# Graph layer 0: gather x itself, put the dense work beside the last quads, write the weighted one-hots on VectorE

## What is computed

```python
qk = x @ Wqk + bqk
v = x @ Wv + bv
scores = jnp.sum(qk[dst] * qk[src], axis=-1) / jnp.sqrt(jnp.float32(D))
scores = jnp.clip(scores, -5.0, 5.0)
e = jnp.exp(scores - m[dst])
s = jax.ops.segment_sum(e, dst, num_segments=N)
attn = e / s[dst]
out = jax.ops.segment_sum(attn[:, None] * v[src], dst, num_segments=N)
out = out @ Wo + bo
h = out + x
...
return gamma * (h - mu) / jnp.sqrt(var + 1e-05) + beta
```

## Time and profile before

| | us |
|---|---|
| three runs | 3143.76 (median), 3142.85, 3181.03 |
| the profiled execution: its own time | 3180.83 |
| its span | 3179.0 |
| first gather of layer 0 / its first score | 50.89 / 67.00 |
| last gather of layer 0 issued | 1297.58 |
| first load of the dense stage | 1312.32 |
| first gather of layer 1 | 1468.88 |

### The profile page before, as it was taken

One profiled execution on the slowest core, in us unless ns is written; L12 is line 12 of the kernel. 1 busy time (PEld: TensorE's weight loads), 2 busy tenths in 40 slices (PEclk: granted clock), 3 DMA queues, 4 the chain that ended last, 5 costly groups with the idle time before them and its releaser, 6 DMA issues. The chain is left out here.

```text
span 3179.0 us, 56851 instructions
## 1 busy us (share of the span) xinstructions
PE 2260.2 (71%) x15187; PEld 1822.2 (57%) x15187; DVE 1546.5 (49%) x6430; ACT 1040.5 (33%) x2916; POOL 1719.9 (54%) x1751
## 2 busy tenths in 40 slices
PE   4666667667667666554677777777777777777879
PEld 4666666657666566543455555555555555555656
DVE  4444444444444444595244444444444444444566
ACT  0222222222222222242244344344344344344443
POOL 2666666666666666445545545545545545545312
PEclk8988888898898988786788888878888878888879
DMA  6555555555555555224444444444444444444301
GB/s 216 159 151 154 152 154 152 153 154 152 154 151 153 153 153 152 68 73 119 132 126 124 127 126 122 129 123 124 129 125 123 129 123 127 127 124 126 109 15 37
DMA packets 443720, 413.11 MB, mean 130 GB/s; under 512 B 72747, under 2 KB 374571, under 8 KB 443532
## 3 DMA queue, kind: packets, MB, share of 16 engines
q1 hardware_dynamic: 356380, 233.60, 26.0%
q0 software_dynamic: 66560, 163.68, 19.3%
q10 hardware_dynamic: 20592, 13.63, 1.3%
HBM read 393.41 MB, written 17.25 MB: 129 GB/s over the span
## 5 line engine op out<-in xcount | busy, mean ns | idle before, releaser
L831 POOL DMA_INDIRECT rows<-xl_tab,src_cols x832 | 800.7, 962 | 730.2 <-DVE message L988 496.7
L254 POOL DMA_INDIRECT rows<-qkv_tab,src_cols x832 | 819.6, 985 | 477.8 <-remote 227.0
L301 PE MATMUL tile_sums<-gather,rows 128*128 128x128 f32 x1664 | 402.6, 330 | 395.3 <-issue 382.9
L301 PEld LDWEIGHTS tile_sums<-gather,rows 128*128 128x128 f32 x1664 | 308.3, 231 | 440.7 <-issue 438.8
L333 DVE CUSTOM_DVE_ANT_0 product<-rows,q_dst 128x128 f32<-128x128 f32 x832 | 234.4, 282 | 626.4 <-remote 567.0
L1001 DVE SCALAR_TENSOR_TENSOR node_sums<-node_sums,shrunk,tile_sums 128x128 f32 x832 | 282.0, 339 | 393.0 <-remote 358.0
L897 PEld LDWEIGHTS z_ps<-spread,window 128*128 128x128 f32 x1664 | 259.5, 215 | 222.6 <-issue 202.1
L303 PE MATMUL tile_sums<-gather,ones 128*128 128x128 f32 x1664 | 380.9, 317 | 0.0
L264 ACT ACTIVATE weight<-clipped 128x4 f32<-128x4 f32 x208 | 42.7, 205 | 954.6 <-issue 590.2
L342 DVE TENSOR_TENSOR node_sums<-node_sums,tile_sums 128x256 f32 x832 | 351.2, 422 | 4.8 <-PE tile_sums L303 1.6
L897 PE MATMUL z_ps<-spread,window 128*128 128x128 f32 x1664 | 272.2, 298 | 93.5 <-issue 88.9
(11 more groups left out here) (154 smaller groups left out, 2626.7 us busy)
## 6 DMA issues: line engine op xcount, KB each, us to landing
rel_bc<-rel_rows SPq DMA_DIRECT2D x416, 128.0 KB
window<-qkv_tab SPq DMA_DIRECT2D x832, 64.0 KB
attr<-in_attrT SPq DMA_DIRECT2D x208, 256.0 KB
window<-xr_tab SPq DMA_DIRECT2D x832, 64.0 KB
rows<-qkv_tab,src_cols POOLq DMA_INDIRECT x832
rows<-xl_tab,src_cols POOLq DMA_INDIRECT x832
qkv_tab<-qkv ACTq DMA_DIRECT2D x13, 512.0 KB, 5.4
xT<-in_xT SPq DMA_DIRECT2D x13, 256.0 KB, 5.1
```

The source lines that it names most:

```text
L254: nc.gpsimd.indirect_dma_start(out=rows[:, q * QT + i, :], out_offset=None, in_=qkv_tab, in_offset=bass.IndirectOffsetOnAxis(ap=src_cols[: ...
L301: nc.tensor.matmul(bank[:, i % 2, 0, :], rows[:, q * QT + i, P:], gather1[:, q % 2, i, :], start=True, stop=True)
L831: nc.gpsimd.indirect_dma_start(out=rows[:, r, i, :], out_offset=None, in_=xl_tab, in_offset=bass.IndirectOffsetOnAxis(ap=src_cols[:, tile: ...
```

## The change

- POOL gathers rows of x, an input (128 floats), into a ring of eight quads; so it can start before any table is made. It waits for `summed`, now raised twice a quad.
- The score of an edge is x[src] . p[dst] + c[dst]. `p_tab` holds p and c, 129 floats a node, from the weights multiplied together once at the start. Windows are 128 x 129.
- The sums are of weighted rows of x; Wv and Wo, multiplied together, are applied later (`w_vo`).
- `onehot_ps` and ACT's scaling are gone. DVE writes `gather1` from `iota_row`, `rel_cols` and the weight in one operation per tile.
- Layer 0 is written out in full on all engines, in steps T. Step T scores quad T, makes the one-hots of T-1 and adds the sums of T-2. `p_dst` and `tile_sums` have one buffer for each half of a quad.
- The table is made in the same block, four blocks ahead of the quads, with ACT copying.
- The dense work of block b begins at step 199 + b. It projects by `w_vo`, with the weights turned by four one-column products; two normalisations stay there; the middle one is folded into the last for the tables (eps changes), and x1 itself is scaled by ACT in layer 1 (`norm_x1`), after the ninth quad, a block a quad.
- In layer 1, several semaphores of DVE's chain are one.

The diff, cut to its core:

```diff
-    qkv_tab = nc.dram_tensor("qkv_tab", (NP, 2 * P), F32).ap()
+    p_tab = nc.dram_tensor("p_tab", (NP, P + 1), F32).ap()
...
+    AHEAD0 = 8
+    SLOTS = 4
+    DENSE = 199
...
+                for Q in range(quads):
+                    r = Q % AHEAD0
+                    if Q >= AHEAD0:
+                        pool.wait_ge(summed, 2 * (Q - AHEAD0 + 1))
+                    for i in range(QT):
+                        tile = Q * QT + i
+                        nc.gpsimd.indirect_dma_start(
+                            out=rows[:, r, i, :], out_offset=None, in_=t["x"],
...
+                def spread_p(Q, k):
+                    if k == 0:
+                        pe.wait_ge(spread_made, Q + 1)
+                        pe.wait_ge(window_in[Q % SLOTS], (Q // SLOTS + 1) * (QT + 1) * DMA)
+                    if Q:
+                        pe.wait_ge(scored, 2 * (Q - 1) + k + 1)
...
+                def add_up(Q, k):
+                    if k == 0:
+                        pe.wait_ge(onehot_made, Q + 1)
+                    if Q:
+                        pe.wait_ge(added, (Q - 1) * QT + 2 * k + 2)
...
+                for T in range(steps):
+                    for k in range(2):
+                        if T + 1 < quads:
+                            spread_p(T + 1, k)
+                        if 0 <= T - 1 < quads:
+                            add_up(T - 1, k)
+                    if T + QUADS < node_groups:
+                        make_p(T + QUADS)
+                    b = T - DENSE
...
+                    if 0 <= b < blocks:
+                        project(b)
+                    if 0 <= b - 5 < blocks:
+                        turn_v(b - 5)
+                        tables(b - 5)
...
+                def make_onehots(Q):
+                    dve.wait_ge(weighted, Q + 1)
...
+                        o = nc.vector.tensor_scalar(gather1[:, Q % 2, i, :], iota_row[:], rel_cols[:, tile:tile + 1],
+                                                    weight[:, Q % 2, i:i + 1], ALU.is_equal, ALU.mult)
...
+                def residual(b):
+                    n = block_tiles(b)
+                    dve.wait_ge(projected, b + 1)
+                    nc.vector.reciprocal(share[:, 0:n], t_ps[:, 0, 0:n]).then_inc(inverted, 1)
...
+                        o = nc.vector.scalar_tensor_tensor(h[:, b % 2, i, :], o_ps[:, i, :], share[:, i:i + 1],
+                                                           x_nm[:, b % QT, i, :], ALU.mult, ALU.add)
...
+                    if T < quads:
+                        clip(T)
...
+                    if 0 <= b - 1 < blocks:
+                        shift0(b - 1)
+                    if 0 <= b - 4 < blocks:
+                        shift1(b - 4)
+                    if 0 <= b < blocks:
+                        residual(b)
+                    if 0 <= b - 3 < blocks:
+                        moments1(b - 3)
+                    if 0 <= b < blocks:
+                        moments0(b)
...
+                def norm_x1(b):
+                    for i in range(block_tiles(b)):
+                        at = b * QT + i
+                        nc.scalar.activation(x1[:, b, i, :], x1[:, b, i, :], ACT.Identity, bias=shift1[:, at:at + 1],
```

More of the change, by code:

```diff
@@ L203, in build @@
[L203 to L211 removed]
+        w_in = sb("w_in", [P, 2, P])
@@ L235, in _ @@
             def _(sp):
-                def body(j, first, last):
-                    for q in range(QUADS):
-                        if not first:
-                            sp.wait_ge(q_spread, j * QUADS + q - QUADS + 1)
-                        sp.dma_start(rel_bc[:, q, :], rel_rows[bass.ds(j * QUADS + q, 1), :].to_broadcast([P, QW])
-                                     ).then_inc(window_in[q], DMA)
-                        for i, base in enumerate(window_bases(sp, j, q), q * QT):
-                            sp.dma_start(window[:, i, :], qkv_tab[bass.ds(base, P), 0:P]).then_inc(window_in[q], DMA)
@@ new lines, in spread_p @@
+                def spread_p(Q, k):
[4 more added lines that the diff above has]
+                        pe.wait_ge(scored, 2 * (Q - 1) + k + 1)
+                    for i in range(2):
+                        at = (2 * k + i) * P
+                        mm = nc.tensor.matmul(p_dst[k][:, i, 0:P + 1], spread[:, Q % 2, at:at + P],
+                                              window[:, Q % SLOTS, 2 * k + i, :], start=True, stop=True)
+                    mm.then_inc(p_spread, 1)
@@ new lines, in add_up @@
+                def add_up(Q, k):
[3 more added lines that the diff above has]
+                        pe.wait_ge(added, (Q - 1) * QT + 2 * k + 2)
+                    for i in range(2):
+                        nc.tensor.matmul(tile_sums[k][:, i, 0, :], rows[:, Q % AHEAD0, 2 * k + i, :],
+                                         gather1[:, Q % 2, 2 * k + i, :], start=True, stop=True)
+                        mm = nc.tensor.matmul(tile_sums[k][:, i, 1, :], ones[:], gather1[:, Q % 2, 2 * k + i, :],
@@ L304, in add_up @@
                                               start=True, stop=True)
                     mm.then_inc(summed, 1)
-                spread_q(0, 0, True)
-                def body(j, first, last):
-                    for q in range(QUADS):
-                        if q < QUADS - 1:
-                            spread_q(j, q + 1, first and q == 0)
-                        elif not last:
-                            spread_q(j + 1, 0)
-                        add_up(j, q, first and q < 2)
-                groups_of(pe, groups, body)
@@ L504, in tables @@
                 def tables(b):
[L506 removed]
+                    pe.wait_ge(hT_made, b + 1)
                     if b:
[L508 to L514 removed]
@@ L515, in _ @@
-                all_steps([(0, project), (3, turn_v), (-1, spread_inverse), (-2, turn_weights), (3, tables)])
+                        pe.wait_ge(lr_kept, b)
+                    for i in range(block_tiles(b)):
+                        nc.tensor.matmul(lr_ps[i // 2][:, i % 2, :], hT[:, i, :], w_lr[:], start=True, stop=False)
+                        mm = nc.tensor.matmul(lr_ps[i // 2][:, i % 2, :], ones[0:1, :], b_lr[:], start=False, stop=True)
+                    mm.then_inc(lr_made, 1)
+                pe.wait_ge(w_loaded, 6 * DMA)
@@ new lines, in _ @@
+                nc.tensor.matmul(lr_ps[0][0:1, 0, P:P + 1], b_in[:, 0:1], b_in[:, 0:1], start=True, stop=True)
+                nc.tensor.matmul(t_ps[:, 2, :], w_turned[:, 1, :], w_out[:], start=True, stop=True)
+                nc.tensor.matmul(lr_ps[0][0:1, 1, 0:P], b_in[:, 1:2], w_out[:], start=True, stop=True).then_inc(m_made, 1)
+                pe.wait_ge(m_kept, 4)
+                for b in range(QUADS):
+                    make_p(b)
+                spread_p(0, 0)
+                spread_p(0, 1)
@@ new lines, in score @@
+                def score(Q, k):
+                    dve.wait_ge(p_spread, 2 * Q + k + 1)
+                    if k == 0:
+                        dve.wait_ge(gathered[Q % AHEAD0], (Q // AHEAD0 + 1) * QT * DMA)
+                        if Q >= 2:
+                            dve.wait_ge(clip_done, Q - 1)
+                    for i in range(2):
+                        o = nc.vector.tensor_tensor_reduce(product[:, 2 * k + i, :], rows[:, Q % AHEAD0, 2 * k + i, :],
+                                                           p_dst[k][:, i, 0:P], 1.0, p_dst[k][:, i, P:P + 1], ALU.mult,
+                                                           ALU.add, scores[:, Q % 2, 2 * k + i:2 * k + i + 1])
+                    o.then_inc(scored, 1)
@@ L674, in build @@
+                dve.wait_ge(added, tiles)
     attention = ExitStack()
@@ L884, in _ @@
                         raise_falls(s)
+                    if Q >= LAG and Q - LAG < blocks:
+                        norm_x1(Q - LAG)
             @block.tensor
```

949 lines of the change are left out of this document (449 added, 500 removed).

## The result

| | before, us | after, us |
|---|---|---|
| median, runs | 3160.94, 4 | 3318.81, 4 (3317.32 to 3327.51) |
| ratio, 95% interval | | 1.0503, 1.0416 to 1.0591 |
| profiled execution / its span | 3180.83 / 3179.0 | 3319.3 / 3317.5 |
| exponential of quads 0 / 9 / 199 (ACT) | 68.2 / 118.7 / 1261.1 | 63.6 / 172.0 / 1301.2 |
| us a quad, quads 20 to 199 | 6.01 | 5.95 |

The four runs of the kernel before lie at 3143 and at 3180 us and its profiled execution is one of the upper pair, which is why the medians are 158 us apart and the two spans 138.

The account below looks back on a forecast made before the run. Gathers holding PE's signals, plus POOL's restart, bound layer 0's loop. Layer 1 starting 64 us earlier, less 10 inside it, gives 54 of 3180.83 (1.7%), which scales the median 3143.76 to 3090; range 3020 to 3200.

Parts of the forecast that it names:

- What bounds the loop: Layer 0's edges: PE's signals wait for POOL's gathers, 1.44 us each; four and a restart make 6.00, forecast 6.05 a quad.
- The 0.05: Layer 0's loop: us a quad added for one-hots on DVE lengthening the gathers beside them, taken between 0 and 0.14.
- the rival of the port: Layer 0's quads: one-hots and gathers fight for a port; 3357 at the locked price, 3190 in milder form; chance 0.20.
- The start: Before layer 0's loop: 32 gathers to 50 us, then table work; first score at 62, ninth quad of gathers about 70.
- 200 quads remain: Loop's end in layer 0: after the ninth quad's gathers at 70, quads at 6.05 each; last burst at 1274.
- The dense work beside quads: Steps 202 to 209, no gathers: eight steps of 10.5 us, 84 in all, to 1376.
- some 2 us: Dense work beside quads: DVE's wait in a step for PE's projection, whose matmuls were put at 0.9.
- The tail: Steps 210 and 211 at 6 us each, then the last block's chain of 16.8; layer 1 starts at 1405.
- The 2.9: Tail: us for the tables in the last block's chain, from 37.3 over 13 blocks.
- Layer 1: Layer 1: `norm_x1` gives ACT 1.65 us in each of 13 quads; could cost 21 or nothing, 10 taken.
- half-paying overlap: Rival: dense steps wait on held or late signals, 14 us not 10.5, and 21 in layer 1; +40, 3129; chance 0.15.

Follow-up runs that it names:

- e9: The changed kernel with POOL gathering three tiles of each quad, not four, from the ninth quad on; 3094.97 us, loop 4.68 us a quad.
- e11: The changed kernel with exponential ahead of copies, no one-row bias products, projection first, dense work from step 210, ring of four quads; 3183.58 us, loop 6.01.
- jobs 1 and 4: Two of five groups of runs, each on one chip; the kernel before took 2502 and 2507 us there, in the others 3177 to 3193.
- e4: The changed kernel with the exponential ahead of the table copies in ACT's order; 2586.99 us, start 61.8 us.
- e7: The changed kernel with the projection ahead of the step's products in PE's order; 3295.30 us, dense part 255 us.
- e5: The kernel before, unchanged, run again for its trace; 3189.22 us.
- e6: The changed kernel, unchanged, run again for its trace; 3354.10 us, in a job where the kernel before took 3193.17.
- e12: The changed kernel with exponential ahead of copies and both biases on DVE, projection still behind the step's products; 3200.23 us, dense part 210 us.
- e1: The changed kernel with the dense blocks from step 210 on, behind all quads; 2632.34 us where the kernel before took 2502.12.
- job 5: A group of runs on one chip, where the kernel before took 3177.18 us.

## Why the prediction was wrong

The forecast of 3090 missed by 229 us, and the sign. Some 36 of these lie between the median that it starts from (3143.76) and the profiled execution (3180.83); the rest, 192, is that layer 1 started 201 us late, less 9 for what the forecast had put on layer 1. By its own steps, in the profiled executions:

- **What bounds the loop**: right. 6.05 forecast, 5.95 measured; the period follows the gathers (e9), the ring's depth does nothing (e11), the one-hots cost nothing that can be seen. The 0.05 that I added for them had the wrong reason too: a gather took 986 ns on the mean before and 956 after, with more work of DVE beside it. Both forms of the rival of the port (3190 and 3357) come nearer to the time than the forecast, by no merit: one-hots stay at 1.11 us beside gathers (they took 3.02 only beside POOL's tensor operations). That signals are held at all isn't universal; jobs 1 and 4 had no such hold, which the text couldn't know.
- **The start**: the first score came at 56.1 (62 forecast, bounds 50 and 72) and the ninth quad of gathers at 73.0 (70). The step that failed is the next: "200 quads remain", each at 6.05 at once. Eight of them took 12.9, some 54 us that stand in no term. I had the four blocks ahead of the loop in the sum and not the nine inside it, whose copies stand ahead of the exponential in ACT's order (e4: 46 us of it).
- **The dense work beside quads**: "10.5 a step", added up on DVE and ACT. From the projection of step 202 to that of step 210 eight steps took 149.5 us, 18.7 each: 65 us more than the 84 forecast.

```profile
1353.50 1.05 PE L319 MATMUL t_ps<-ones,node_sums 1*128 1x1 f32 x8
...
1503.01 1.70 PE L319 MATMUL t_ps<-ones,node_sums 1*128 1x1 f32 x8
```

  I gave PE "0.9" for the projection; it took 5.1, as L323 has a second product for each, t_ps comes first, and the clock was 0.60. The wait of DVE for it was put at "some 2 us" and was 8.0 at step 200: PE had the quad's 5.4 us ahead of it in its order (moved by e7: 55 us, of which 20 in steps 199 to 203). From step 204 on PE also has the tables, 9.2 us a block, which the term left out.
- **The tail**: 29 us from step 210 to layer 1, with one block's chain. It took 104: the tables come five steps behind the projection, so seven blocks of them follow one another there, 12 to 16 us apart. The 2.9 that I took for a block of tables was of one product for each tile, at the mean clock of before; two products at 0.50 are 9.2.
- **Layer 1**: +10 for `norm_x1`; measured +1 in the result's pair and +29 between e5 and e6. That stretch took 1696 to 1713 us in three executions of the kernel before alone, so the size of this term stays open.

Together: 3 for the ninth quad, 54, less 20 for the loop's 0.1 a quad, 24 in steps 199 to 201, 65 and 75, which are the 201 us by which layer 1 started late. (They are differences of times of one trace, so that they add up proves nothing; the sizes that experiments moved are 46 for ACT's order, 59 and 41 for the bias products and 55 for PE's order, and 164 for all four at once.) The misses of the dense work and of the tail have one mistake in common: the stage was summed on the engine that was busiest before (DVE), and PE's new work was never counted instruction by instruction, though the kernel has a second product on each line. The miss of the start is another one, an item ahead of a more urgent one in an engine's order, which no sum of busy times shows. The rival that should have stood there, with its condition, is "PE becomes the bound of the dense blocks"; of those that I named, half-paying overlap was the nearest (14 us a step).

On the clock the Trainium skill, "TensorE: Matmul & The Clock Gate", section "What's actually happening", says that the gate follows how busy TensorE has been recently. The overlap's windows agree (76% busy at 0.61, 96% at 0.71). The steps with tables hardly do (89% at 0.61, 94% at 0.75), and the stretch from 1500 to 1520 doesn't: 19 of 20 us busy, and 0.50 throughout. No run here shows what kept it down.

## What to carry to other kernels

When work is moved onto an engine that has room by its share, count what it gets per step, instruction by instruction, at the clock of that stage and not of the loop: here a one-row bias product cost as much as the full product that it follows. In a step written out for several engines, look in each engine's order for an item that waits on another engine, and ask who needs what stands behind it; two swaps of order (e4, e7) were worth 46 and 55 us here, the second 23 once the products around it were fewer (e12). And measure an overlap by undoing it: here it brought nothing as written, and 12 us when mended.

## What the runs showed of the hardware

- In three of the five jobs and in the profiles of the result, engines that wait for TensorE move late while POOL's gathers are out, and the pace is 1.44 us a gather: bursts of 3, 4, 8 and 24 gathers all fit (4.63 less the restart, 5.75, 11.5, 34.2). That TensorE's signals are held is the reading of these times; in the burst of 24 some came through on the way. In the other jobs the same kernels show no hold, and POOL issues a gather each 1.26 us:

```profile
706.91 0.95 POOL L253 DMA_INDIRECT rows<-in_x,src_cols  x1 [0.31 <-issue]
708.17 0.95 POOL L253 DMA_INDIRECT rows<-in_x,src_cols  x1 [0.30 <-issue]
```

  These rows are e1's, in job 1, with a quad each 5.0 us and the whole kernel before at 2502 and not 3180 us. What differs between the jobs stays open; the record has chip number 1 both for job 1, without the hold, and for job 5, with it.
- A float32 product whose weights have one row took 710 ns on the mean where the one with 128 rows took 715 (256 columns, L340 and L339), and 402 where that took 399 (128 columns).
- TensorE's granted clock was 0.52 over the last 157 us of the dense work, while it was busy 82% of them, and 0.51 over 264 us of e1 at 85%.
- Four float32 `tensor_scalar` operations of VectorE on 128x128 took 1.10 to 1.13 us in all of 180 quads, beside gathers that GpSimd issues; beside GpSimd's tensor operations the same four took 3.02 us once in the changed kernel and 2.05 to 5.07 in e7.
